# Linear attention's read-out: TensorE and VectorE in an order that spans three batches

## The reference

```python
data_dash = einsum('bhnd,md->bhnm', data_normalizer * data, proj)
diag_data = sum(square(data), -1) * 0.5 * data_normalizer ** 2
stab = max(data_dash, -1) if is_query else max(data_dash)
features = ratio * (exp(data_dash - diag_data - stab) + EPS)      # q1 from q, k1 from k
kv = einsum('bhnm,bhnd->bhmd', k1, v);  ksum = sum(k1, axis=2)
z = 1.0 / einsum('bhnm,bhm->bhn', q1, ksum)
out = einsum('bhnm,bhmd->bhnd', q1, kv) * z[..., None]
h = h + (out @ W_proj + b_proj)
```

## Time and profile before

| | us |
|---|---|
| median of 3 runs | 2577.85 (2576.46 to 2578.14) |
| profiled execution | 2583.43 |
| its span | 2581.4 |
| TensorE busy in the span | 1948.3 |
| VectorE busy | 1506.0 |
| ScalarE busy | 1060.0 |

### The profile page before, as it was taken

The page is one execution under the profiler, slowest core; times in us unless marked ns, Lnnn a source line. Parts: engine busy times, 40 slices in busy tenths (PEclk is TensorE's granted clock), DMA queues, the critical chain, the costliest instruction groups (busy, mean ns, idle before and its releaser), DMA issues. The chain is left out here.

```text
span 2581.4 us, 31194 instructions
## 1 busy us (share of the span) xinstructions
PE 1948.3 (75%) x9560; PEld 1011.4 (39%) x9560; DVE 1506.0 (58%) x2508; ACT 1060.0 (41%) x1847; POOL 405.8 (16%) x592
## 2 busy tenths in 40 slices
PE   5687888868876351777568865788899994899994
PEld 4555645444334120000111123333123332788883
DVE  6376378843003665999757774788968886111113
ACT  2001122222111356999878863222167762222221
POOL 5000000000111000111100002522103335122221
PEclk9899989966886565555589986777589997899997
DMA  3011100051992003433000102977767742566664
GB/s 79 18 31 38 46 23 16 11 222 58 392 411 108 12 0 96 145 118 118 25 18 25 36 0 53 126 110 104 94 79 92 97 61 71 176 204 203 204 204 182
DMA packets 147741, 265.16 MB, mean 103 GB/s; under 512 B 28618, under 2 KB 115883, under 8 KB 142636
## 3 DMA queue, kind: packets, MB, share of 16 engines
q1 hardware_dynamic: 135996, 242.54, 36.3%
q0 software_dynamic: 10480, 18.04, 2.1%
q10 hardware_dynamic: 1152, 3.15, 0.3%
HBM read 221.85 MB, written 57.71 MB: 108 GB/s over the span
## 5 line engine op out<-in xcount | busy, mean ns | idle before, releaser
L1646 PE MATMUL ps<-arena 128*128 x384 | 195.8, 615 | 122.1 <-DMA arena<-arena 62.2
L1680 ACT ACTIVATE ps<-ps,arena 128x512 f32<-128x512 f32 x384 | 257.0, 1456 | 7.7 <-POOL arena L1666 7.7
L2091 DVE TENSOR_REDUCE arena<-ps 128x1024 f32 x192 | 227.7, 1222 | 50.4 <-PE ps L2241 44.4
L1656 DVE TENSOR_REDUCE arena<-ps 128x1024 f32 x192 | 234.7, 1226 | 38.1 <-PE ps L1646 22.1
L1680 ACT ACTIVATION_READ_ACCUMULATOR ps<-ps,arena 128x1 f32 x384 | 239.8, 1002 | 0.0
L2443 ACT ACTIVATE arena<-ps 128x1024 f32<-128x1024 f32 x192 | 185.2, 1022 | 95.7 <-PE ps L2325 94.6
L1830 ACT ACTIVATE arena<-ps 128x1024 f32<-128x1024 f32 x192 | 187.5, 1024 | 33.6 <-DVE arena L1852 29.4
L2773 DVE TENSOR_TENSOR arena<-ps,arena 128x384 f32<-128x384 f32 x39 | 21.8, 558 | 286.8 <-PE ps L2729 286.8
L2241 PE MATMUL ps<-arena 96*128 96x512 bf16 x384 | 159.6, 509 | 37.7 <-DVE arena L2091 25.6
L2753 ACT ACTIVATE arena<-ps,arena 128x256 f32<-128x256 f32 x234 | 89.7, 482 | 235.7 <-PE ps L2718 235.7
L528 PE MATMUL ps<-arena 96*128 96x456 f32 (+1 forms) x512 | 177.2, 500 | 9.6 <-DMA arena<-arena 6.1
(11 more groups left out here) (379 smaller groups left out, 3301.4 us busy)
## 6 DMA issues: line engine op xcount, KB each, us to landing
arena<-in_sm_w_dram SPq DMA_DIRECT2D x128, 576.0 KB
arena<-in_re_w_dram SPq DMA_DIRECT2D x39, 1252.0 KB, 5.9
arena<-ra_parts SPq DMA_DIRECT2D x192, 192.0 KB, 9.8
routed_in<-routed_in SPq DMA_DIRECT2D x8, 3332.0 KB, 14.3
ra_parts<-arena SPq DMA_DIRECT2D x48, 192.0 KB, 2.5
arena<-routed_in SPq DMA_DIRECT2D x39, 196.0 KB, 5.3
arena<-la_xt SPq DMA_DIRECT2D x16, 384.0 KB, 3.4
arena<-arena SPq DMA_DIRECT2D x64, 96.0 KB, 2.2
```

Of the source, the lines that this page charges most:

```text
L1646: ins = pe.matmul(ps[:, 2 * (n % 4) + t % 2, :], QM[j][:, h, t * P:(t + 1) * P], KI[:, b, h // HG, :], start=True, stop=True)
L1656: v.tensor_reduce(MXq[:, b, 2 * u:2 * u + 2, at_head(h)], ps[:, 2 * (n % 4):2 * (n % 4) + 2, :], AX.X, ALU.max).then_inc(s_lk, 1)
L1680: ins = act.activation(bank, bank, ACT.Exp, bias=nb[n % 4][:, t % 2:t % 2 + 1], scale=c_reg, accum_out=RS[:, b, t, at_head(h):at_head(h) + 1])
L2091: v.tensor_reduce(MX[:, bass.ds(b, 1), 2 * (n % 2):2 * (n % 2) + 2, n // 2].rearrange("p o t -> p (o t)"), ps[:, 2 * (n % 2):2 * (n % 2) + ...
```

## The change

The same steps run with the same sizes; their order and two waits differ. TensorE's order for batch b becomes P0(b), T3(b-1), projection(b-2), P1(b), RO0(b-1), T0(b), P2(b), T1(b), P3(b), RO1(b-1), T2(b). VectorE's becomes C0(b), A(b-2), C1(b), N0(b-1), C2(b), C3(b), N1(b-1). Batches 0 and 1 are written out ahead of the loops, and behind the loops come T3(7), projection(6), RO0(7), RO1(7), projection(7), and A(6), N0(7), N1(7), A(7). KX gets semaphores of its own (xk), for which TensorE waits ahead of RO0.

```diff
     xq = [sem(f"la_q_rows{j}_loaded") for j in range(2)]
+    xk = [sem(f"la_k_v_rows{j}_loaded") for j in range(2)]
...
-                                 KVA[:, bass.ds(b, 1)].rearrange("p o w a k d -> p (o w a k d)")).then_inc(xq[j], 16)
+                                 KVA[:, bass.ds(b, 1)].rearrange("p o w a k d -> p (o w a k d)")).then_inc(xk[j], 16)
...
-            def batch(b, behind):
+            def batch(b, behind, last_behind):
                 link = Link(v, s_qk, b * (4 * T))
                 chain(b, link, 0)
+                if last_behind:
+                    add(b - 2)
                 chain(b, link, 1)
                 if behind:
                     normalise(b - 1, 0)
                 chain(b, link, 2)
+                chain(b, link, 3)
                 if behind:
                     normalise(b - 1, 1)
-                chain(b, link, 3)
-                if behind:
-                    add(b - 1)
-
-            batch(0, False)
-            with v.Fori(1, B) as b:
-                batch(b, True)
+
+            batch(0, False, False)
+            batch(1, True, False)
+            with v.Fori(2, B) as b:
+                batch(b, True, True)
+            add(B - 2)
             normalise(B - 1, 0)
             normalise(B - 1, 1)
             add(B - 1)
...
-            def batch(b, i, j, behind):
-                pe.wait_ge(xq[j], 32 * (i + 1))
-                for t in (0, 1):
-                    products(pe, b, j, t, 0, qd, qp)
+            def batch(b, i, j, behind, last_behind):
+                pe.wait_ge(xq[j], 16 * (i + 1))
+                products(pe, b, j, 0, 0, qd, qp)
                 if behind:
+                    turn(b - 1, 3)
+                if last_behind:
+                    project(b - 2)
+                products(pe, b, j, 1, 0, qd, qp)
+                if behind:
+                    pe.wait_ge(xk[1 - j], 16 * (i + j))
                     read_out(b - 1, 1 - j, 0)
                 turn(b, 0)
                 products(pe, b, j, 2, 0, qd, qp)
+                turn(b, 1)
+                products(pe, b, j, 3, 0, qd, qp)
                 if behind:
                     read_out(b - 1, 1 - j, 1)
-                turn(b, 1)
-                products(pe, b, j, 3, 0, qd, qp)
                 turn(b, 2)
-                if behind:
-                    project(b - 1)
-                turn(b, 3)
...
+            batch(0, 0, 0, False, False)
+            batch(1, 0, 1, True, False)
+            with pe.Fori(1, B // 2) as i:
+                for j in range(2):
+                    batch(2 * i + j, i, j, True, True)
+            turn(B - 1, 3)
+            project(B - 2)
+            pe.wait_ge(xk[1], 16 * (B // 2))
             read_out(B - 1, 1, 0)
             read_out(B - 1, 1, 1)
             project(B - 1)
```

## The result

| | before | changed |
|---|---|---|
| median, 7 runs each | 2577.85 us | 2564.03 us |
| lowest and highest | 2572.29, 2583.54 | 2555.58, 2567.40 |
| ratio, 95% interval | | 0.9946, 0.9933 to 0.9960 |
| profiled execution, its span | 2583.43, 2581.4 | 2566.83, 2564.8 |
| first DMA of the read-out to its last statistics | 220.9 | 201.2 |

Forecast were 2559.0 and a gain of 18.9 us. The read-out itself gained 19.7 us in the profile; 13.8 us arrived in the medians of the first chip, 18.0 in those of the second. The period is the time from one C0 to the next.

What follows compares the result with a forecast made beforehand. Bound by waits between TensorE and VectorE, neither full. Gains 0.6+11.1+13.1 less 5.9 give 18.9 us: 2583.43 profiled becomes 2564.5, the median 5.6 lower, 2559.0 us; likeliest 2554 to 2563, with the half clock staying 2553 to 2569.

Steps and rivals of the forecast that it cites:

- The steady state: Batches from the third on: a period of 21.75 us, five of them gaining 13.1 us.
- The ring of waits: In each batch neither engine is full; VectorE waits 0.60 us for the projection and 2.02 us for q products.
- The start: First two batches: batch 1's first q products go ahead of batch 0's last transposes; a gain of 11.1 us.
- The first wait: Before the first q products, which no longer wait for KX: 0 to 1.0 us shorter, taken as 0.6.
- The end: Last batch to last statistics: read-out queued behind the previous batch's projection and stream update; loss of 5.9 us, between 3.4 and 7.8.
- What was costed at nothing: Moved DMA waits, VectorE's loop edges, the new KX wait and written-out batch: 0 us; edges possibly 0 to 1.7 us.
- The sum for the block: Whole read-out block: 0.6+11.1+13.1-5.9, a gain of 18.9 us.
- The later stages only move forward: Blocks behind the read-out: they only shift earlier, so the whole 18.9 us gain reaches the total time.
- likeliest case: Whole kernel: the forecast itself holds, with 70% chance and a time of 2554 to 2563 us.
- rival A: TensorE's half clock stays in the steady state, costing 2 to 5 us over six batches: 2561 to 2564 us; 17%.
- Rival B: Half clock over the projection and second q products in every batch, 5.1 us each: 2584.5 us, slower; 3%.
- Rival C: No steady overlap: q products late or loop edges long, period stays 24.4 us, total 2572 us; 7%.

Runs made afterwards that it cites:

- the two kernels with the old order at full clock: Kernel before with four identity matmuls between P2 and RO1: 0.9994; kernel before with identity matmuls only at the soft MoE's start: 0.9998; both have a 23.7 us period.
- second look: The unaltered changed kernel run again beside the kernel before on a second chip: 2561.93 against 2579.97 us, 0.9932.
- one-semaphore kernel: Changed kernel with KX counted on the semaphore of XTs again, so P0 waits for both: 0.9961 of the kernel before, read-out 207.3 us.

## Why the prediction was right, step by step

- **The steady state** was forecast with 21.75 us and is 21.52. A waits 0.41 us (0.47 forecast), C0 for nothing. The 0.2 us that C1 should lose to P1 did not appear: I put the whole 2.59 us of P1 behind the projection's end, while it starts 0.2 us before that end (464.85, with A at 465.2). The ring of waits named at the outset was the right one; the two kernels with the old order at full clock show that the order carries 2.2 of the 2.5 us. From C0(2) to C0(7) the gain was forecast with 13.1 us and is 14.3.
- **The start** was forecast with 14.35 us from C0(0) to C0(1) and 19.7 from there to C0(2), a gain of 11.1. The first profile has 15.54 and 20.2, a gain of 9.4; the second look and all other kernels with this order of the start that have the split semaphore have 14.3 and 19.7 to 20.0. In the first profile P1(0) ran at half clock (C1(0) waits 2.11 us for it, 0.35 in the second look): the clock at the start was not in my working, only in its range, and T3(0) stands at 335.35 instead of 334.7.
- **The first wait** fell by 1.0 us, the upper end of my range, and by 1.1 in the second look; I had taken 0.6.
- **The end** was forecast 5.9 us longer and is 4.9 longer: projection(6) ran part of its time at half clock (4.68 us to A, between the 3.04 and 5.52 of the working), RO0(7) at full clock, the rest at half as before. In the second look nearly the whole projection(6) ran at half clock (5.40 us to A), and the end is 5.5 longer.
- **What was costed at nothing** cost nothing: VectorE's loop edge is invisible between N1 and C0, and TensorE never waits for XTs in the steady state.
- **The sum for the block**, 18.9 us, came out as 19.7 in the first profile and 21.0 in the second (220.9-199.9). That the first is so near is in part luck: its start gained 1.7 us less than forecast, and the first wait, the steady state and the end together 2.6 more.
- **"The later stages only move forward"** was the loose step: the medians gained 13.8 and 18.0 us, both less than the read-out did, and a single execution varies by some 10 us there. Whether the later stages pass on the whole gain is not shown. The measured 2564.03 lies 5.0 us above the forecast, inside the range. It lies 1 us above the likeliest case, in the part that the range had for rival A, though A did not happen; that it is still inside is luck of the later stages and not a merit of the working.
- **Rival A** did not happen in the changed kernel (clock 1.00 from batch 1 into batch 7), and the one-semaphore kernel shows how near it is. The argument for it, a half clock in every batch after a gap of 2 us, was true of one execution only: with the same read-out and the same gap the clock stayed at 1.00 in another. **Rival B** did not happen at all in the batches. **Rival C**'s period of 24.4 us is near what the late projection does by itself (23.9), though there A waits and C0 hardly does; the late RO1 and N1 by themselves give 27.3.

## What to carry to other kernels

When two in-order engines wait for each other once in a batch, look for the step whose result nobody needs in this batch (here the projection and its stream update) and let it come a batch later, together with the steps that it would otherwise stand in front of; check each half of such a move alone before crediting it. Where an engine has slack, ask what its clock does in the idle time: 1.2 us of waiting inside a slack of 1.7 still cost 1.4 us, in every second batch. And the end of such a loop deserves an order of its own, since the buffers that forced the order inside it are free there.

## What the runs showed of the hardware

- The same waits can leave TensorE's clock at either level. In the one-semaphore kernel P0 took 4.38 us behind waits of 1.12 and 1.24 us, and 2.68 us in the next batch behind 1.12 and 1.21. In the old order the wait of 2.07 us ahead of RO1 was followed by a clock of 0.50 in one execution and of 1.00 in another.
- RO1, with half the matmuls of RO0, takes as long: 1.91 against 1.92 us at full clock, 3.63 and 3.64 at half.
- A reciprocal of 512 columns takes 3.35 us on 128 and 3.34 us on 64 partitions, so the second half of the heads pays the full price; in the changed kernel the two take 6.7 of the 21.5 us of a batch.
